# Flags times edge weights, moved from VectorE to ScalarE column by column, in the sort that runs beside the gathers

## The chip, the cores and the metric

The kernel runs on one core of a Trainium2 chip. The metric is the device time of one execution in microseconds (us). Before the change the median of three runs is 1511.99 us (1509.66 to 1513.52). Engines are named as the profile names them: PE (TensorE), PEld (its weight loads), DVE (VectorE), ACT (ScalarE), POOL (GpSimd), SP (SyncE).

## The reference

A graph layer over 6250 nodes of 256 features and 106,250 weighted edges is followed by an attention block. The part that matters here is the edge sum:

```
support = layernorm(x) @ W;  r_D = sigmoid(support @ a2);  gated = r_D * support
msg = gated[dst] * edge_weight[:, None]
out = segment_sum(msg, src, N);  sumnorm = segment_sum(edge_weight * r_D[dst], src, N)
out = out / sumnorm[:, None]     # then leaky/elu, residual, layernorm, sliced attention
```

## The kernel before

**Whole.** The 6250 rows of `gated` are written to DRAM (`gated_rows_dram`) in 49 blocks of 128. The edges are sorted on the chip into 49 buckets by their target block. Then, tile by tile (128 edges), POOL issues an indirect DMA that gathers 128 rows of 257 numbers, and PE multiplies them with a selection matrix S that holds the edge weights. Every bucket has at first six "head" tiles (294 in all), and later its remaining ones.

**The sort.** The 832 edge columns (128 edges each) are worked in 26 groups `g` of 32 columns, each in two halves `h` of 16. For a group:

- DVE `flag(g)`: an 0/1 matrix `flags4[g%2]` in bf16 that says for each edge and each of 49 buckets whether it belongs there. It lies bucket by bucket, with 34 elements (68 bytes) from one bucket to the next for a fixed edge column.
- PE `above(g)`: counts over the partitions; ACT `front(g)` (L1360) copies them back into the flags; DVE `ranks`, `counts`; PE `quads`, `total`; DVE `quad`.
- DVE `values(g, h)` (L845): for each of 16 columns `hot_v[h][:, j, 0, :]` = flags times the packed index (source and row), and `hot_v[h][:, j, 1, :]` = flags times the edge weight. These are two instructions of 16x49 = 784 elements a half, four a group.
- DVE `hot(g, h)` (L885): the one-hot rank matrix `hot_s[h]`.
- PE `put(g, h)`: 16 products `hot_v` x `hot_s` into a bank (32 matmul records of 128x80 in the profile).
- ACT `runs_out(g)` (L1367) copies the bank out, and POOL `send(g, 0)` and `send(g, 1)` (L664) write it to the sorted list in DRAM.

**The stretch "beside the gathers".** From group G1 + 1 = 7 on, the first 280 head tiles are gathered and summed while the sort goes on, 14 or 15 per group. Nothing is scheduled at run time: each engine has a written order, and the semaphores tie them.

- POOL in group g: 9 gathers (L676), `send(g-1, 0)`, 4 gathers, `send(g-1, 1)`, the rest of the gathers.
- PE in group g (below T0 to T3 are four shares of 3 or 4 gathered tiles): T0, `quads(g)`, `total(g)`, `above(g+1)`, T1, `put(g, 0)`, T2, `put(g, 1)`, T3.
- DVE in group g: `ranks(g)`, `counts(g)`, `flag(g+1)`, `place(g-1)` (L893, waits until `send(g-2, 0)` has landed), S matrices, a copy of indices and weights to PSUM (L1029), `values(g, 0)`, S, `values(g, 1)`, `quad`, `hot(g, 0)`, S, `hot(g, 1)`, S.
- ACT in group g: `runs_out(g-1)`, then for each share T0 to T3 `evac`: when the third tile of a bucket is summed, a copy of the bank (L1411), and behind it ACT itself issues the DMA that stores the sum (L1413). From tile 147 on, that is from group 17 on, it also issues the load of an older sum (L1417), and PE adds that sum back with two more matmul records. After T0, ACT does `front(g+1)`.

PE may start a new sum only when the bank two sums back has been copied out (`s_evac`). A gather into one of 18 row slots waits for the sum of the tile that used it (`s_seg`).

After `send(25, 1)` SP loads the sorted lists, and POOL gathers all the other tiles (L757) to the end of the graph layer.

Of the kernel before, what the change touches and what calls it, by code (L numbers as in the profile page):

```python
# [28 lines left out]
ACT = mybir.ActivationFunctionType  # L29
# [24 lines left out]
GC = 32  # L54
HC = GC // 2
# [4 lines left out]
G1 = 6  # L60
# [41 lines left out]
def build(nc, x, src, dst, ew, W, a1, a2, W_fx, b_fx, W_x, b_x, W_slice, b_slice, W_q, W_k, W_v,  # L102
          W_out, b_out, temp, out, gtab, srt, ovs):
    with ExitStack() as ctx:
# [3 lines left out]
        def sem(name):  # L108
            return ctx.enter_context(nc.semaphore(name))
# [32 lines left out]
        packew = carve(2 * EC)  # L142
        packf, ewf = packew[:, 0:EC], packew[:, EC:2 * EC]
# [39 lines left out]
        hot_v = [carve(HC * VB).rearrange("p (j v b) -> p j v b", v=2, b=NB) for k in range(2)]  # L183
# [4 lines left out]
        flags4 = [halved(t) for t in flags]  # L188
# [5 lines left out]
        vals2 = bank[4][:, 0:2 * GC].rearrange("p (v j) -> p v j", j=GC)  # L194
# [51 lines left out]
        zcol = sb("zcol", [P, 1])  # L246
# [83 lines left out]
        s_flag = sem("s_flag")  # L330
# [8 lines left out]
        s_quad = sem("s_quad")  # L339
        s_hs = sem("s_hs")  # L340
        s_hv = sem("s_hv")
        s_put = sem("s_put")
        s_out = sem("s_out")
        s_run = sem("s_run")
# [174 lines left out]
        def share(g, late):  # L519
            lo, hi = (max(0, n - late) for n in early[g])  # L520
            cuts = [lo + (hi - lo) * i // 4 for i in range(5)]
            return [range(cuts[i], cuts[i + 1]) for i in range(4)]
# [260 lines left out]
        def _(dve):  # L783
            step = Chain(dve, s_dve)
            v = nc.vector
# [42 lines left out]
            def flag(g):  # L828
                k = g % 2
                if g >= 2:  # L830
                    dve.wait_ge(s_base, g - 1)
                step(v.tensor_tensor(flags4[k][:, :, :, 1:HS],
                                     hib[:, g * GC:(g + 1) * GC].rearrange("p (h j) -> p h j", h=2).unsqueeze(1)
                                     .broadcast_to([P, NB, 2, HC]),
                                     buckets, ALU.is_equal))
                v.tensor_tensor(folded[k], flags4[k][:, :, :, 1:HC // 2 + 1], flags4[k][:, :, :, HC // 2 + 1:HS],
                                ALU.add).then_inc(s_flag, 1)

            def values(g, h):
                k = g % 2  # L840
                if g:
                    dve.wait_ge(s_put, g * 2 + h - 1)
                for i, t in enumerate((packf, ewf)):
                    w = vals2[:, i, h * HC:(h + 1) * HC] if g > G1 + 1 else t[:, g * GC + h * HC:g * GC + (h + 1) * HC]
                    m = v.tensor_tensor(hot_v[h][:, :, i, :],  # L845
                                        flags4[k][:, :, h, 1:HS].rearrange("p b j -> p j b"),
                                        w.unsqueeze(2).broadcast_to([P, HC, NB]), ALU.mult)
                m.then_inc(s_hv, 1)
# [164 lines left out]
            for g in range(2, NG):  # L1013
                tiles = share(g, SLAG) if g >= G1 else [()] * 4
                if g == G1 + 1:
                    for k in range(4):
                        dve.wait_ge(s_gd[k], 16 * len(range(k, NB, 4)))
                    decode1(0, CH * KA, 0)
                    step(v.tensor_copy(reset2, reset[:, 0:25 * HS]))
                ranks(g)  # L1020
                pair(g, 0)
                counts(g)
                if g + 1 < NG:
                    flag(g + 1)
                place(g - 1)
                pair(g, 1)
                select1(tiles[0])
                if g > G1 + 1:
                    step(v.tensor_copy(vals2, packew.rearrange("p (v n) -> p v n", v=2)[:, :, g * GC:(g + 1) * GC]))  # L1029
                values(g, 0)  # L1030
                pair(g, 2)
                select1(tiles[1])
                values(g, 1)
                pair(g, 3)
                quad(g)
                hot(g, 0)
                select1(tiles[2])
                pair(g, 4)
                hot(g, 1)
                pair(g, 5)  # L1040
                if g == 4:
                    bias()
                if g == G1 + 1:
                    decode1(CH * KA, NB * KA, 1)
                if g == G1 + 8:
                    decode1(NB * KA, NT1, 2)
                select1(tiles[3])
# [17 lines left out]
            for i in range(2):  # L1065
# [4 lines left out]
                m = v.tensor_scalar(neededi[:, 2 * i + 1, :], sumf, 16.0, None, ALU.mult)  # L1070
# [210 lines left out]
            for c in range(2):  # L1281
                m = v.tensor_scalar(Mn[:, c, :], bank[2 + c // 2][:, (c % 2) * F:(c % 2 + 1) * F], nrm[:, 1, c:c + 1], None,
                                    ALU.mult)
# [32 lines left out]
            for lo in (0, G):  # L1316
                m = v.tensor_tensor(ad[lo:lo + G, :, lo:lo + G], al[lo:lo + G, :, :],
                                    nrm[lo:lo + G, 2, :].unsqueeze(2).broadcast_to([G, NP2, G]), ALU.mult)
# [25 lines left out]
        def _(act):  # L1344
            a = nc.scalar
            a.preload_act_table_set("natural_log_exp_and_others")
            step = Chain(act, s_act)
# [7 lines left out]
            def front(g):  # L1355
# [3 lines left out]
                    act.wait_ge(s_cp, g - 1)  # L1359
                a.copy(flags4[k][:, :, :, 0], bank[0][:, 0:2 * NB].rearrange("p (b h) -> p b h", h=2)).then_inc(s_bs, 1)  # L1360

            def runs_out(g):
                k = g % 2
                act.wait_ge(s_put, g * 2 + 2)
                if g >= 2:
                    act.wait_ge(s_run, g * 32 - 32)
                a.copy(runs[k], run_bank(g)[0:VB, 0:2 * RUN]).then_inc(s_out, 1)  # L1367
# [35 lines left out]
            def evac(ns):  # L1403
                for n in ns:
                    if n % KA == KA - 1:
                        i = n // KA
                        k = i % 2
                        act.wait_ge(s_seg, n + 1)
                        if i >= 2:
                            act.wait_ge(s_pd[k], 16 * (i // 2))  # L1410
                        a.copy(ovr[:, k, :], bank[6 + k][:, 0:GW]).then_inc(s_evac, 1)  # L1411
                        act.wait_ge(s_evac, i + 1)
                        act.dma_start(ovs[:, i % NB, :], ovr[:, k, :]).then_inc(s_pd[k], 16)  # L1413
                        b = i - (NB - 3)
                        if 0 <= b < NB:
                            act.wait_ge(s_pd[b % 2], 16 * (b // 2 + 1))
                            act.dma_start(back[b % 3], ovs[:, b, :]).then_inc(s_back[b % 3], 16)  # L1417
# [10 lines left out]
            for i in range(3):  # L1428
                m = a.copy(bxc3[:, :, i], bxc[:, :])
# [14 lines left out]
            for g in range(G1 + 1, NG):  # L1444
                runs_out(g - 1)
                for i, ns in enumerate(share(g, LAG)):
                    evac(ns)
                    if i == 0 and g + 1 < NG:
                        front(g + 1)
# [66 lines left out]
            for c in range(2, NP2):  # L1516
                m = a.activation(Mn[:, c, :], bank[3][:, (c % 2) * F:(c % 2 + 1) * F], ACT.Identity, bias=zcol[:, 0:1],
                                 scale=nrm[:, 1, c:c + 1])
# [29 lines left out]
        def _(pe):  # L1548
# [24 lines left out]
            def put(g, h, lo=0, hi=HC):  # L1573
                if lo == 0:
                    pe.wait_ge(s_hv, g * 2 + h + 1)
                    pe.wait_ge(s_hs, g * 2 + h + 1)
                for j in range(lo, hi):
                    m = mm(run_bank(g)[0:VB, h * RUN:(h + 1) * RUN], hot_v[h][:, j, :, :].rearrange("p v b -> p (v b)"),
                           hot_s[h][:, j, :], j == 0, j == HC - 1)
                if hi == HC:  # L1580
                    m.then_inc(s_put, 1)
# [65 lines left out]
            for k in range(2):  # L1647
                for c in range(NP2):
                    t = nc.tensor.transpose(bank[6 + k][:, c * P:(c + 1) * P], Wxr[:, k, c // 2, (c % 2) * P:(c % 2 + 1) * P], ident[:, :])
                t.then_inc(s_wxt, 1)  # L1650
            pe.wait_ge(s_wxc, 3)
            for c in range(NP2):
                for k in range(2):
                    mm(bank[4 + k][:, c * P:(c + 1) * P], WxT[:, c, k * P:(k + 1) * P], Ws2[:, :])
                m = mm(bank[3][0:3, c * P:(c + 1) * P], bxc3[:, c, :], Ws2[:, :])
# [46 lines left out]
            with pe.If_ne(slow, 0):  # L1702
# [9 lines left out]
                for c in range(2):  # L1712
                    w = OV // 2
                    m = mm(bank[1 + c][0:1, 0:w], ones[0:NB, 0:1], ge[0:NB, c * w:(c + 1) * w])
# [118 lines left out]
            for c in range(NP2):  # L1833
                for f in range(2):
                    nc.tensor.transpose(bank[4 + f][:, c * P:(c + 1) * P], Mn[:, c, f * P:(f + 1) * P], ident[:, :])
                t = nc.tensor.transpose(bank[6][0:1, c * P:(c + 1) * P], nrm[:, 2, c:c + 1], ident[:, :])
# [3 lines left out]
            for c in range(NP2):  # L1840
# [4 lines left out]
                m = mm(o, bfx[:, cs], nbT[:, cs], False, True)  # L1845
# [3 lines left out]
            for c in range(NP2):  # L1849
                mm(bank[4][:, c * P:(c + 1) * P], W3[:, 0, :], tokd[:, c, :])  # L1850
                mm(bank[5][:, c * G:(c + 1) * G], W3[:, 1, :], tokc[:, c, :])
                m = mm(bank[6][:, c * P:(c + 1) * P], tokd[:, c, :], W3[:, 2, :])
# [3 lines left out]
            for c in range(NP2):  # L1856
                m = mm(bank[7][:, c * G:(c + 1) * G], qd[:, c, :], kc[:, c, :])
# [3 lines left out]
            for c in range(NP2):  # L1861
                t = nc.tensor.transpose(bank[4][:, c * P:(c + 1) * P], ad[:, c, :], ident[:, :])
# [3 lines left out]
            for c in range(NP2):  # L1866
                m = mm(bank[5][:, c * P:(c + 1) * P], vd[:, c, :], aT[:, c, :])
# [3 lines left out]
            for c in range(NP2):  # L1871
                m = mm(bank[6 + c // 2][:, (c % 2) * F:(c % 2 + 1) * F], oT[:, c, :], Wo[:, c, :])
# [46 lines left out]
```

## Time and profile before

| | us |
|---|---|
| median of 3 runs | 1511.99 |
| profiled execution | 1510.68 |
| its span | 1508.9 |
| PE busy in the span | 1215.9 |
| DVE busy | 1084.6 |
| ACT busy | 387.3 |
| POOL busy | 907.6 |

The profile cuts the span in 40 slices of 37.7 us. The sort beside the gathers fills slices 6 to 17 (about 195 to 640 us). "Busy" of POOL is the time of its DMA instructions, with 0.3 us between two of them that is booked as "issue". PE works at one of two clocks, 1.2 and 2.4 GHz; the profile shows the granted clock as a fraction of the higher one (0.50 or 1.00, or a mean of both over a stretch).

### The profile page before, as it was taken

To read this page: it belongs to the slowest core of one execution; us is meant where nothing else is said; L and a number is where in the kernel's file an instruction comes from. 1 tells how busy PE (TensorE), PEld (TensorE's weight loads), DVE (VectorE), ACT (ScalarE), POOL (GpSimd) and SP (SyncE) were. 2 spreads that over 40 slices of the span, in tenths; PEclk is the share of its full clock that TensorE was granted. 3 is DMA by queue.
4 is the path that set the end of the run, shared out by engine and by line. 5 is a ranking of instruction groups with operands and counts; after the bars stand their busy time and mean duration, and the time that the engine had idled before them with its cause. 6 is when DMAs were issued, how large, how long until landed. Compare 5 with 4: busy or idle time off the path is not lost.

```text
span 1508.9 us, 21356 instructions
## 1 busy us (share of the span) xinstructions
PE 1215.9 (81%) x6049; PEld 894.5 (59%) x6049; DVE 1084.6 (72%) x2779; ACT 387.3 (26%) x1221; POOL 907.6 (60%) x920
## 2 busy tenths in 40 slices
PE   4198867778788888768888888888888888888998
PEld 3187666567677777534555455545545555456787
DVE  8976799999989998435776766767676677665322
ACT  1066500111111111001332332333233333323232
POOL 0110167777777777767777777777777777770000
PEclk9599878898898989878999998999999999999999
DMA  8011144446455555556444445444444444441022
GB/s 260 2 51 61 59 66 122 120 123 126 122 148 144 153 148 162 150 117 121 111 116 115 113 116 114 117 113 114 114 111 116 113 116 116 111 112 50 23 75 72
DMA packets 158676, 166.45 MB, mean 110 GB/s; under 512 B 84287, under 2 KB 129235, under 8 KB 158572
## 3 DMA queue, kind: packets, MB, share of 16 engines
q0 software_dynamic: 42848, 114.59, 28.8%
q1 hardware_dynamic: 94556, 31.24, 9.0%
q10 hardware_dynamic: 21168, 19.35, 4.2%
q8 instruction: 50, 0.82, 0.2%
q14 instruction: 54, 0.44, 0.1%
HBM read 136.73 MB, written 28.38 MB: 109 GB/s over the span
## 4 chain that ended last, share of the span: by engine, by line
PE 30%; POOL 22%; DMA 16%; issue 14%; DVE 13%; POOLq 2%; SPq 1%; ACT 1%; DVEq 0%; ACTq 0%
PE bank L1550 29%; POOL rows L757 16%; DMA rows<-gated_rows_dram,ring_i 10%; POOL rows L676 6%; DVE big L845 5%; DMA sorted_edges_dram<-big,idx 4%; DVE big L885 2%; DMA res<-in_x_dram 2%; POOLq L749 2%; DVE S L1010 1%; DVE big L854 1%; SPq L545 1%; DVE big L858 0%; DVE big L959 0%; DVE big L872 0%
## 5 line engine op out<-in xcount | busy, mean ns | idle before, releaser
L1550 PE MATMUL bank<-rows,S 128*128 128x257 f32 (+1 forms) x2254 | 643.1, 408 | 133.7 <-DMA rows<-gated_rows_dram,ring_i 107.8
L757 POOL DMA_INDIRECT rows<-gated_rows_dram,ring_i x564 | 541.4, 960 | 178.0 <-issue 154.5
L1550 PEld LDWEIGHTS bank<-rows,S 128*128 128x128 f32 x2254 | 408.0, 197 | 327.1 <-DMA rows<-gated_rows_dram,ring_i 205.4
L676 POOL DMA_INDIRECT rows<-gated_rows_dram,lg x294 | 297.6, 1012 | 97.3 <-issue 75.9
L1550 PE MATMUL bank<-big 128*98 128x80 f32 (+2 forms) x1741 | 200.9, 283 | 96.8 <-DVE big L885 90.6
L1550 PEld LDWEIGHTS bank<-big 128*98 128x98 f32 (+1 forms) x1741 | 196.2, 201 | 110.3 <-issue 108.1
L1178 DVE TENSOR_SCALAR S<-iota,lof,srec 128x128 f32<-128x128 f32 x637 | 177.9, 351 | 1.5 <-PE bank L1550 1.3
L664 POOL DMA_INDIRECT sorted_edges_dram<-big,idx x52 | 67.7, 1302 | 178.7 <-ACT big L1367 94.8
L1189 DVE TENSOR_TENSOR ag<-bank,ovr 128x257 f32<-128x257 f32 x49 | 20.9, 428 | 196.0 <-PE bank L1550 196.0
L1411 ACT COPY ovr<-bank 128x257 f32<-128x257 f32 x98 | 36.7, 374 | 326.7 <-PE bank L1550 323.1
L1550 PE MATMUL bank<-Wxs,xT 128*128 128x512 f32 x196 | 111.5, 697 | 0.1
L845 DVE TENSOR_TENSOR big<-big,bank 128x784 f32<-128x784 bf16 x72 | 107.3, 1531 | 0.6
L1550 PE MATMUL bank<-xn,lg 128*128 128x256 f32 x392 | 101.5, 383 | 0.0
L1550 PE MATMUL bank<-big,lg 128*128 128x128 bf16 (+4 forms) x492 | 63.7, 282 | 46.6 <-issue 25.7
L1456 ACT ACTIVATE bc<-bc 128x1 f32<-128x1 f32 x49 | 9.9, 203 | 309.1 <-DVE bc L1218 309.1
L1010 DVE TENSOR_SCALAR S<-iota,lg,srec 128x128 f32<-128x128 f32 x294 | 83.3, 356 | 0.8 <-issue 0.8
L1550 PEld LDWEIGHTS bank<-xn,lg 128*128 128x128 f32 x392 | 75.8, 194 | 10.8
L1550 PEld LDWEIGHTS bank<-big,lg 128*128 128x128 bf16 x492 | 40.9, 106 | 62.8 <-issue 26.6
L1496 ACT ACTIVATE big<-bank,zcol 128x128 f32<-128x128 f32 (+1 forms) x196 | 68.2, 357 | 1.4 <-PE bank L1550 1.4
L858 DVE TENSOR_TENSOR_SCAN big<-bank,big 128x425 bf16<-128x425 f32 x72 | 67.7, 1002 | 0.0
L1334 DVE TENSOR_TENSOR S<-bank,res 128x256 f32<-128x256 f32 x49 | 20.8, 424 | 64.6 <-PE bank L1550 64.6
L1550 PEld LDWEIGHTS bank<-Wxs,xT 128*128 128x128 f32 x196 | 37.2, 210 | 40.7 <-issue 40.3
(236 smaller groups left out, 1369.8 us busy)
## 6 DMA issues: line engine op xcount, KB each, us to landing
overflow_sums_dram<-ovr ACTq DMA_DIRECT2D x98, 128.5 KB
rows<-gated_rows_dram,ring_i POOLq DMA_INDIRECT x564, 2.8
gated_rows_dram<-rows SPq DMA_DIRECT2D x49, 128.5 KB, 2.6
ovr<-overflow_sums_dram SPq DMA_DIRECT2D x49, 128.5 KB
res<-in_x_dram SPq DMA_DIRECT2D x1, 6144.0 KB
out_dram<-S SPq DMA_DIRECT2D x48, 128.0 KB, 1.7
rows<-gated_rows_dram,lg POOLq DMA_INDIRECT x294, 3.0
xn<-overflow_sums_dram ACTq DMA_DIRECT2D x33, 128.5 KB, 3.0
```

The source lines that it names most:

```text
L664: pool.indirect_dma_start(srt[:, :], bass.IndirectOffsetOnAxis(ap=idx[:, k, h:h + 1], axis=0), runs[k][:, h * RUN:(h + 1) * RUN], None).th ...
L676: pool.indirect_dma_start(rows[:, turn(n), :], None, gtab[:, :], bass.IndirectOffsetOnAxis(ap=ring1[:, n:n + 1], axis=0)).then_inc(s_row[t ...
L749: return pool.to_reg(pool.value_load(neededi[0:1, i, b:b + 1], min_val=0, max_val=1))
L757: pool.indirect_dma_start(rows[:, slot(b, u), :], None, gtab[:, :], bass.IndirectOffsetOnAxis(ap=ring_i[:, b // CH % 2, n:n + 1], axis=0)) ...
L845: m = v.tensor_tensor(hot_v[h][:, :, i, :], flags4[k][:, :, h, 1:HS].rearrange("p b j -> p j b"), w.unsqueeze(2).broadcast_to([P, HC, NB]) ...
L858: m = v.tensor_tensor_scan(run[:, lo * HS:lo * HS + n], reset2[:, 0:n], flags[k][:, lo * HS:lo * HS + n], 0.0, ALU.mult, ALU.add)
L885: v.tensor_tensor(hot_s[h], r.unsqueeze(2).broadcast_to([P, HC, RUN]), iota1[:, 0:RUN].unsqueeze(1).broadcast_to([P, HC, RUN]), ALU.is_equ ...
L1010: v.tensor_scalar(S[:, turn(n), :], iota[:, :], lof1[:, n:n + 1], srec[:, 1, n:n + 1], ALU.is_equal, ALU.mult).then_inc(s_S, 1)
L1178: v.tensor_scalar(S[:, S_slot(b, u), :], iota[:, :], lof[:, b // CH % 2, n:n + 1], srec[:, 1, NT1 + b * TQ + u:NT1 + b * TQ + u + 1], ALU. ...
L1411: a.copy(ovr[:, k, :], bank[6 + k][:, 0:GW]).then_inc(s_evac, 1)
L1496: m = a.activation(swt[:, c, b * P:b * P + n], bank[7][:, c * P:c * P + n], ACT.Identity, bias=zcol[:, 0:1], accum_out=nacc[:, c, b:b + 1])
L1550: return nc.tensor.matmul(o, l, r, start=start, stop=stop, skip_group_check=True)
```

## The change

From group 7 on, `values` makes only the product with the packed index on DVE. The product with the edge weight is made by ACT in `weighted(g, lo, hi)`, 8 columns ahead of each `evac`, so 32 instructions of 128x49 a group. Each reads one column of flags (49 elements, 68 bytes apart) and writes 49 contiguous f32, with two per-partition operands: the weight as scale and a zero column as bias. A new semaphore `s_he` counts finished halves; PE's `put(g, h)` waits for it, and DVE's `flag(g)` waits for it before it writes over the flags. The copy to PSUM takes the indices alone.

```diff
             def flag(g):
                 if g >= 2:
                     dve.wait_ge(s_base, g - 1)
+                if g - 2 > G1:
+                    dve.wait_ge(s_he, (g - 2 - G1) * 2)
...
             def values(g, h):
-                for i, t in enumerate((packf, ewf)):
+                for i, t in enumerate((packf, ewf)[0:1 if g > G1 else 2]):
...
-                    step(v.tensor_copy(vals2, packew.rearrange("p (v n) -> p v n", v=2)[:, :, g * GC:(g + 1) * GC]))
+                    step(v.tensor_copy(vals2[:, 0, :], packf[:, g * GC:(g + 1) * GC]))
...
+            def weighted(g, lo, hi):
+                k = g % 2
+                for n in range(lo, hi):
+                    h, j = divmod(n, HC)
+                    if n == lo:
+                        act.wait_ge(s_flag, g + 1)
+                    if j == 0 or n == lo:
+                        act.wait_ge(s_put, g * 2 + h - 1)
+                    m = a.activation(hot_v[h][:, j, 1, :], flags4[k][:, :, h, 1 + j], ACT.Identity, bias=zcol[:, 0:1],
+                                     scale=ewf[:, g * GC + n:g * GC + n + 1])
+                    if j == HC - 1:
+                        m.then_inc(s_he, 1)
...
             for g in range(G1 + 1, NG):
                 runs_out(g - 1)
                 for i, ns in enumerate(share(g, LAG)):
+                    weighted(g, i * 8, i * 8 + 8)
                     evac(ns)
...
             def put(g, h, lo=0, hi=HC):
                     pe.wait_ge(s_hv, g * 2 + h + 1)
                     pe.wait_ge(s_hs, g * 2 + h + 1)
+                    if g > G1:
+                        pe.wait_ge(s_he, (g - G1 - 1) * 2 + h + 1)
```

ACT's order in a group of the first half, before; L1367 is `runs_out`, L1360 `front`, and L1411 with L1413 one copied and stored sum:

```order
L1367 COPY big<-bank1 98x160 [waits s_run,s_put]
L1411 COPY ovr<-bank6 128x257 [waits s_pd0,s_seg]
L1413 DMA overflow_sums_dram<-ovr 128x257 [waits s_evac]
L1360 CAST big<-bank0 128x98 [waits s_cp,s_base]
L1411 COPY ovr<-bank7 128x257 [waits s_pd1,s_seg]
L1413 DMA overflow_sums_dram<-ovr 128x257 [waits s_evac]
L1411 COPY ovr<-bank6 128x257 [waits s_pd0,s_seg]
L1413 DMA overflow_sums_dram<-ovr 128x257 [waits s_evac]
L1411 COPY ovr<-bank7 128x257 [waits s_pd1,s_seg]
L1413 DMA overflow_sums_dram<-ovr 128x257 [waits s_evac]
```

The same group after the change, where the lines are 3 and 16 higher (L1383 `runs_out`, L1363 `front`, L1427 and L1429 the sum) and L1373 is `weighted`:

```order
L1383 COPY big<-bank1 98x160 [waits s_run,s_put]
L1373 ACTIVATE big<-big,zcol 128x49 [waits s_put,s_flag]
L1373 ACTIVATE big<-big,zcol 128x49 x7
L1427 COPY ovr<-bank6 128x257 [waits s_pd0,s_seg]
L1429 DMA overflow_sums_dram<-ovr 128x257 [waits s_evac]
L1363 CAST big<-bank0 128x98 [waits s_cp,s_base]
L1373 ACTIVATE big<-big,zcol 128x49 [waits s_put,s_flag]
L1373 ACTIVATE big<-big,zcol 128x49 x7
L1427 COPY ovr<-bank7 128x257 [waits s_pd1,s_seg]
L1429 DMA overflow_sums_dram<-ovr 128x257 [waits s_evac]
L1373 ACTIVATE big<-big,zcol 128x49 [waits s_put,s_flag]
L1373 ACTIVATE big<-big,zcol 128x49 x7
```

Eight columns now stand ahead of the first, second and third copy, and (past the end of the piece) eight more ahead of the last.

PE's order around the two `put` of a group, after the change (before, the two rows with `s_he` wait for `s_hs,s_hv` alone):

```order
L1567 MATMUL bank<-big 98x80 [waits s_he,s_hs,s_hv]
L1567 MATMUL bank<-big 98x80 x15
L1567 MATMUL bank<-rows,S 128x257 [waits s_S,s_row12,s_evac]
L1567 MATMUL bank<-rows,S 128x257 [waits s_S,s_row13]
L1567 MATMUL bank<-rows,S 128x257 [waits s_S,s_row14]
L1567 MATMUL bank<-rows,S 128x257 [waits s_S,s_row15,s_evac]
L1567 MATMUL bank<-big 98x80 [waits s_he,s_hs,s_hv]
L1567 MATMUL bank<-big 98x80 x15
```

Nothing moves on PE: T2 stands between `put(g, 0)` and `put(g, 1)` as before, and each `put` has one more semaphore to wait for.

## Rows read from the trace of the kernel before

**Rows 1.** The page, part 2: POOL busy in tenths, 40 slices.
```profile
POOL 0110167777777777767777777777777777770000
```
**Rows 2.** Waits of POOL, 240 to 660 us: us in total, times, longest.
```profile
POOL rows L676 <- issue: 70.1, 230, 0.3
```
**Rows 3.** Waits of DVE and of PE, 240 to 660 us.
```profile
DVE idx L893 <- DMA sorted_edges_dram<-big,idx: 34.2, 15, 7.0
...
PE bank L1550 <- DVE big L885: 60.0, 17, 5.6
```
**Rows 4.** Timeline: start us, us, engine, line; first and last `runs_out`, last `send` pair.
```profile
221.47 0.29 ACT L1367 COPY big<-bank 98x160 f32<-98x160 f32 x1 [2.38 <-PE bank L1550]
...
618.98 0.29 ACT L1367 COPY big<-bank 98x160 f32<-98x160 f32 x1 [1.17 <-issue]
...
628.03 0.99 POOL L664 DMA_INDIRECT sorted_edges_dram<-big,idx  x1 [0.30 <-issue]
```
**Rows 5.** Groups by line and shape, DVE and PE, 250 to 850 us.
```profile
L1550 PE MATMUL bank<-big 128*98 128x80 f32 x1088 | 131.9, 295 | 60.0 <-DVE big L885 60.0
...
L845 DVE TENSOR_TENSOR big<-big,bank 128x784 f32<-128x784 bf16 x66 | 98.3, 1531 | 0.5
...
L885 DVE TENSOR_TENSOR big<-bank,lg 128x1280 f32<-128x1280 f32 x34 | 50.4, 1481 | 0.0
```
**Rows 6.** ACT by line and shape; the first by its own line, min/median/max ns; a timeline pair.
```profile
L1373 ACT ACTIVATE rows<-res,big x49: 583/590/652, 58.2 to 176.7; 128x256 f32<-128x256 f32 x49
...
151.14 1.08 ACT L1373 ACTIVATE rows<-res,big 128x256 f32<-128x256 f32 x2
...
L1411 ACT COPY ovr<-bank 128x257 f32<-128x257 f32 x94 | 35.2, 374 | 314.5 <-PE bank L1550 310.9 <-DMA overflow_sums_dram<-ovr 2.6
...
L1360 ACT CAST big<-bank 128x98 bf16<-128x98 f32 x16 | 9.4, 588 | 42.5 <-PE bank L1550 42.5
...
L1493 ACT COPY big<-bank 128x88 f32<-128x88 f32 x1 | 0.2, 232 | 2.5 <-PE bank L1550 2.5
```
**Rows 7.** PE's timeline, one late group, from behind one `put(g-1, 1)`.
```profile
485.39 1.07 PE L1550 MATMUL bank<-rows,S 128*128 128x257 f32 x4
...
494.64 2.97 PE L1550 MATMUL bank<-big 128*98 128x80 f32 x32 [0.73 <-DVE big L885]
497.45 0.64 PE L1550 MATMUL bank<-ag,ident 128*128 128x257 f32 x2
...
500.10 2.92 PE L1550 MATMUL bank<-big 128*98 128x80 f32 x32
```
**Rows 8.** ACT's timeline in the same group.
```profile
487.81 0.29 ACT L1367 COPY big<-bank 98x160 f32<-98x160 f32 x1 [0.94 <-ACT ovr L1411]
...
500.20 0.45 ACTq L1417 DMA_DIRECT2D ag<-overflow_sums_dram  x1
```
**Rows 9.** PE's and ACT's timeline, one early group.
```profile
243.13 3.25 PE L1550 MATMUL bank<-rows,S 128*128 128x257 f32 x14
...
245.06 0.29 ACT L1367 COPY big<-bank 98x160 f32<-98x160 f32 x1 [0.45 <-ACT ovr L1411]
...
245.95 0.33 ACTq L1413 DMA_DIRECT2D overflow_sums_dram<-ovr  x1
```
**Rows 10.** A slower `put` behind a wait, and the clock granted in it and in a later one.
```profile
474.39 5.59 PE L1550 MATMUL bank<-big 128*98 128x80 f32 x32 [4.12 <-DVE big L885]
...
474.50:480.00 5.50, 5.50 (x33) 5.50 (x34) 5.50 (x11) 0.00 (x0) 4.14 (x5) 0.50 0.38 102
500.20:502.80 2.60, 2.60 (x33) 2.60 (x32) 2.57 (x5) 0.00 (x0) 1.99 (x3) 1.00 0.69 196
```
**Rows 11.** Timeline of group 7, and POOL's gathers by shape, 250 to 850 us.
```profile
205.33 3.43 POOL L676 DMA_INDIRECT rows<-gated_rows_dram,lg  x1 [0.30 <-issue]
...
205.00 2.98 DVE L845 TENSOR_TENSOR big<-big 128x784 f32<-128x784 bf16 x2
...
L676 POOL DMA_INDIRECT rows<-gated_rows_dram,lg x266 | 259.4, 975 | 81.0 <-issue 69.1 <-PE bank L1550 6.1 <-DMA sorted_edges_dram<-big,idx 4.3
```

More of the change, by code:

```diff
@@ L341, in build @@
         s_hv = sem("s_hv")
+        s_he = sem("s_he")
         s_put = sem("s_put")
```

## The prediction

> **What bounds the kernel now.** I read the page first, then the waits of the stretch in which the sort runs beside the gathers, then one group of it in the order of time.
>
> POOL is busy seven tenths in nearly every slice from the start of the gathers to the end of the graph layer [rows 1]. The rest is not waiting: in 240 to 660 us the idle time ahead of its gathers is 0.3 us between any two, 230 times, put down to "issue" [rows 2]. So POOL issues without a pause, and what another engine does more quickly changes nothing unless POOL was waiting for it. DVE itself is held by POOL: 34.2 us it waits for a `send` to land [rows 3]. PE waits 60.0 us, 17 times, for `hot` [rows 3], about 3.5 us a group. It runs ahead of POOL, though: `runs_out(25)` stands at 618.98, and POOL comes to `send(25, 0)` only at 628.03 [rows 4]. So PE and ACT can fall back by 9.0 us before POOL waits for them at the end of the sort. From 221.47, `runs_out(7)`, to 618.98 are 18 groups, 22.08 us each [rows 4]. Break-even is therefore a ring of PE and ACT of 22.08 + 9.0/18 = **22.6 us a group**. Everything behind the sort waits for the last `send` and shifts with it.
>
> **What the change takes away.** Two of four `values` instructions a group, 1531 ns each [rows 5]: 3.1 us of DVE in 19 groups, 58 us in all, and a shorter copy. For the time this is worth nothing in groups 8 to 25, since DVE already waits for POOL; it waits longer in `place`, and `hot` is ready 3 us earlier. In group 7 alone both operands of `values` lie in SBUF, and one gather issued beside it took 3.43 us where the mean is 0.975 [rows 11]. Two instructions less there give POOL back about 2 x 1.5 = 3 us. They might also give nothing (other work fills the gap).
>
> The skill's page on SBUF (Trainium skill, "SBUF — State Buffer", section "SBUF: two separate sides") says that DVE with two SBUF inputs and GpSimd share a port pair that one holds for its whole instruction. The slow gather beside `values` agrees; by that rule, too, groups 8 and later give nothing, because one operand is in PSUM there.
>
> **What it adds on ACT.** 32 instructions a group. The trace has no such one, so I bound it. A pair of L1373 (256 elements, SBUF to SBUF, scale and bias per partition) takes 1.08 us, one 0.59, so 0.49 from start to start [rows 6]. An element costs (374 - 232)/(257 - 88) = 0.84 ns [rows 6]. With 49 elements instead of 256: 0.49 - 207 x 0.84 ns = **0.32 us**, the lower end, if the 68-byte steps cost nothing. For the steps there are two rows. DVE reads the same flags in L845 at 1531/784 = 1.95 ns an element, against 1481/1280 = 1.16 in L885 [rows 5]: 0.8 ns more, over 49 elements 0.04 us, so 0.36 us. ACT itself writes bf16 34 bytes apart in L1360: 588 ns for 98 elements, where 232 + 10 x 0.84 = 240 would be due [rows 6]. That is 3.55 ns an element, over 49 elements 0.17 us, so **0.49 us**, the upper end. I take 0.36, since that row reads these very data; L1360 writes. Eight columns (call them W) then take 8 x 0.36 + 0.1 for the end = 3.0 us; at the ends 2.65 and 4.05.
>
> The same page of the Trainium skill, in its box on cachelines, says that SBUF has 16-byte lines and that each access in a new line pays a penalty, which here is every element. It gives no price; the two rows agree that there is one. Without it the sum would go by 0.32, with it by more.
>
> In work alone ACT has room: 32 x 0.36 = 11.5 us and some 7 of its own in 22 (five copies with their issues at 1.25, `front` 0.6, `runs_out` 0.3). What counts is the order: ACT makes the last eight columns only after it has copied a sum out of T2, which PE has only after `put(g, 0)`, and PE cannot begin `put(g, 1)` before.
>
> **The ring, late groups (17 to 25)** [rows 7, 8], counted from 485.39, when `put(g-1, 1)` is done:
> - `runs_out` ends at 488.10: +2.7. First W: 5.7.
> - Copy and two DMA issues: 0.37 + 0.33 + 0.45 and 0.1 of gaps = 1.25 [rows 6, 8, 9]: 7.0. `front` 0.59, 0.1 of it overlapped [rows 6]: 7.5. Second W: 10.5. PE had T1 behind it at 494.64 - 0.73 = 493.91, +8.5, so it now waits 2.0.
> - `put(g, 0)` 497.45 - 494.64 = 2.8: 13.3. T2 500.10 - 497.45 = 2.65: 15.95.
> - The copy of T2 and its issues end at 500.65, 0.55 behind T2: 16.5. Last W and a semaphore: 19.6. PE waits 3.65.
> - `put(g, 1)` 2.8: **22.4 us**.
>
> That is with PE at full clock. The `put` behind a wait of 4.12 us took 5.59 us at a granted clock of 0.50 (1.2 GHz); one without a wait took 2.92, in a stretch at 1.00 [rows 10]. Over the 34 `put` of rows 5, two a group cost 131.9/17 = 7.76 us, so the one behind the wait 4.84, 1.9 more than the other. The wait for `hot` goes; a wait of 3.65 us before the other `put` takes its place, and 2.0 before the first. I add 1.9 once: **24.3 us**.
>
> **Early groups (8 to 16)** [rows 9], from 243.13: `runs_out` ends at +2.2, W 5.2, copy with one issue 0.8: 6.0, `front` 6.5, W 9.5, `put` 12.3, T2 four tiles at 3.25/7 = 0.46, 14.1, tail at most 0.55, W and semaphore 17.7, `put` 20.5, with the slower clock **22.4 us**.
>
> **Sum.** Lag behind the old pace of 22.1: 9 x 0.3 + 9 x 2.2 = 22.5 us, less the 9.0 of lead: 13.5 us. The 3 us of group 7 don't come off, because PE and ACT then set the end of the sort, not POOL. 1510.68 + 13.5 = 1524.2; the median of the runs lies 1.3 above the profiled execution: **1525 us**. DVE's new wait in `flag(g+2)` for the last eight columns of g holds its `place`, S matrices and `values(g+1)` up to near the end of `put(g, 1)`. Of these the two `values` are 3.1 us [rows 5], and I estimate the rest at as much again; PE wants `hot(g+1, 0)` only 10 us after that `put`, so I count it as nothing; were that cover gone, it would add up to 1 us a group.
>
> **Rivals.**
> - **POOL stays the bound** (other side: no change). If eight columns take 2.65, the ring is 1.05 less: 21.4 and 23.3, a lag of 9 x 1.2 = 11 against 9.0; if the waits don't lower the clock, late groups take 22.4 and lag 3. The sort then ends at POOL's pace, less 3 us from group 7 at best: 1509 to 1514. It decides at 22.6 us a group. For it: waits of PE are only moved, and the lead in the middle of the sort is larger than at its end. Against it: two waits a group where there was one.
> - **Strided reads cost ACT what its strided writes cost.** W is 4.05, three of them are in the ring: +3.15. Early 25.6, late 27.5, lag 9 x 3.5 + 9 x 5.4 = 80, less 9.0: 1510.68 + 71 + 1.3 = 1583. For it: the only strided row of ACT. Against: that is a 2-byte write, and DVE's read pays far less.
> - **DVE's relief reaches POOL everywhere.** If each of the 266 gathers of rows 11 became 3% shorter and the ring stayed under 22.6, that is 8 us: 1504. For it: POOL is the bound and group 7 shows that DVE can slow it. Against: the removed instructions read one operand from PSUM from group 8 on.
>
> **How the numbers follow.** Forecast 42% (own range 1515 to 1545, about half a microsecond a group either way), POOL stays the bound 26%, dear strided reads 25%, relief of POOL 7%. A difference under 0.3% (4.5 us) can't be told from no change. Faster is the last case: 0.07. No change is most of the first rival: 0.24. Slower is the rest: 0.69. The range is 1507 to 1585: it leaves out the relief and the upper half of the dear reads beyond 1583, under 2 in 10.
>
> **What would show it.** Right: 608 new ACT instructions of 0.45 to 0.5 us in the profile, 0.36 from start to start; PE waits for ACT instead of `hot`, twice a group and longer before `put(g, 1)`; `runs_out` 23 to 24 us apart in late groups; POOL waits for ACT or PE ahead of the last `send`, which comes some 13 us later; the stretch behind it unchanged in length. Wrong: POOL still with nothing but "issue" ahead of it, or columns at 0.5 us from start to start, or DVE as the one that PE waits for.

## The result, and the profile after

The changed kernel takes 1561.97 us (median of 4 runs, 1560.64 to 1564.36), the kernel before 1511.45 beside it: ratio 1.0324, 95% interval [1.031, 1.0337]. It is 50.5 us slower where the forecast was 13.5. In the profile of the changed kernel the lines of `values`, `hot` and `put` are L848, L888 and L1567, `runs_out` is L1383, a copied sum L1427, its DMA issues L1429 and L1433, `send` L665, and `weighted` L1373.

The waits in 200 to 720 us of the kernel after (engine and line, what it waited for, us in total, times, longest); they answer to [rows 2, 3], which cover 240 to 660 us of the kernel before:

```profile
POOL rows L677 <- issue: 68.6, 225, 0.3
POOL rows L677 <- PE bank L1567: 62.6, 55, 5.5
POOL sorted_edges_dram L665 <- ACT big L1383: 9.7, 1, 9.7
...
PE bank L1567 <- ACT big L1373: 118.5, 38, 5.1
...
DVE big L835 <- ACT big L1373: 83.5, 17, 7.1
```

POOL, which stood no longer than 0.3 us before any of these gathers [rows 2], now waits 62.6 us for PE, up to 5.5 at a time, and 9.7 for the last `runs_out`. PE waits for ACT, twice a group, instead of for `hot`. DVE, which waited 34.2 us for a `send` to land, now stands 83.5 us in `flag`, behind ACT's columns.

The new instructions, by their own line (min/median/max ns), and the first, a middle and the last `runs_out` of the stretch with the last `send(25, 0)`; they answer to [rows 4, 6]:

```profile
L1373 ACT ACTIVATE big<-big,zcol x608: 451/455/498, 201.5 to 669.4; 128x49 f32<-128x49 bf16 x152
...
225.30 0.29 ACT L1383 COPY big<-bank 98x160 f32<-98x160 f32 x1 [5.77 <-PE bank L1567]
...
440.31 0.29 ACT L1383 COPY big<-bank 98x160 f32<-98x160 f32 x1 [0.45 <-ACT ovr L1427]
...
679.10 0.29 ACT L1383 COPY big<-bank 98x160 f32<-98x160 f32 x1 [1.10 <-issue]
...
680.39 0.99 POOL L665 DMA_INDIRECT sorted_edges_dram<-big,idx  x1 [9.74 <-ACT big L1383]
```

`runs_out(25)` stands at 679.10 instead of 618.98, 60.1 us later; `send(25, 0)` at 680.39 instead of 628.03, 52.4 us later; the span is 53.7 longer. So the loss is made in the sort, and the rest of the kernel is little more than shifted. The nine early groups took (440.31 - 225.30)/9 = 23.9 us each, the nine late ones (679.10 - 440.31)/9 = 26.5.

One late group on PE and on ACT, from behind `put(g-1, 1)` at 514.36; it answers to [rows 7, 8]:

```profile
514.36 1.62 PE L1567 MATMUL bank<-rows,S 128*128 128x257 f32 x4
...
524.99 2.97 PE L1567 MATMUL bank<-big 128*98 128x80 f32 x32 [1.56 <-ACT big L1373]
...
530.57 0.60 PE L1567 MATMUL bank<-rows,S 128*128 128x257 f32 x2
536.21 5.59 PE L1567 MATMUL bank<-big 128*98 128x80 f32 x32 [5.04 <-ACT big L1373]
541.59 1.66 PE L1567 MATMUL bank<-rows,S 128*128 128x257 f32 x4
```
```profile
517.33 0.29 ACT L1383 COPY big<-bank 98x160 f32<-98x160 f32 x1 [0.94 <-ACT ovr L1427]
517.52 2.99 ACT L1373 ACTIVATE big<-big,zcol 128x49 f32<-128x49 bf16 x8
...
521.85 2.99 ACT L1373 ACTIVATE big<-big,zcol 128x49 f32<-128x49 bf16 x8
524.75 0.35 ACT L1427 COPY ovr<-bank 128x257 f32<-128x257 f32 x1
...
526.04 0.38 ACT L1427 COPY ovr<-bank 128x257 f32<-128x257 f32 x1 [0.94 <-ACT ovr L1427]
526.44 1.85 ACTq L1429 DMA_DIRECT2D overflow_sums_dram<-ovr  x1
528.33 0.45 ACTq L1433 DMA_DIRECT2D xn<-overflow_sums_dram  x1
528.88 2.99 ACT L1373 ACTIVATE big<-big,zcol 128x49 f32<-128x49 bf16 x8 [2.47 <-PE bank L1567]
531.78 0.35 ACT L1427 COPY ovr<-bank 128x257 f32<-128x257 f32 x1
...
533.08 2.99 ACT L1373 ACTIVATE big<-big,zcol 128x49 f32<-128x49 bf16 x8 [0.95 <-ACT ovr L1427]
```

Up to 525 us this is the forecast: the second eight columns end 10.5 us after `put(g-1, 1)`. Then the third eight begin only at 528.88, behind two copied sums with their four issues (one of them 1.85 us). PE has finished T2 at 531.2, but the copy out of T2 starts at 531.78, when those eight are through. The last eight end at 536.07, and `put(g, 1)` then runs at the lower clock.

This group is one of the slower ones. In three late groups of the nine the issue of one stored sum took 1.43, 1.85 and 1.88 us on ACT instead of 0.33, and there 11.0 to 11.3 us pass from the start of `put(g, 0)` to that of `put(g, 1)`. Four late groups have neither such an issue nor a slow `put(g, 0)`. In three of them ACT has three copied sums between its second and its last eight columns, and they need 9.7 us, as this one:

```profile
605.27 2.97 PE L1567 MATMUL bank<-big 128*98 128x80 f32 x32 [2.00 <-ACT big L1373]
...
614.98 5.59 PE L1567 MATMUL bank<-big 128*98 128x80 f32 x32 [4.53 <-ACT big L1373]
```

In the fourth (`put(18, 0)` at 475.08) only two copied sums lie there, and it needs 8.4 us.

The steps of the ring over all groups, as means of nine in us, read from PE's timeline of the kernel after as in the prediction (each step from start to start), with the prediction's own sums beside them:

| step | early, forecast | early, measured | late, forecast | late, measured |
|---|---|---|---|---|
| end of `put(g-1, 1)` to `put(g, 0)` | 9.5 | 9.53 | 10.5 | 10.99 |
| `put(g, 0)` | 2.8 | 4.38 | 2.8 | 3.27 |
| from there to `put(g, 1)` | 5.4 | 5.65 | 6.3 | 7.13 |
| `put(g, 1)` | 4.7 | 4.04 | 4.7 | 5.05 |
| whole ring | 22.4 | 23.60 | 24.3 | 26.43 |

Between two `runs_out` it is 23.9 and 26.5, since `runs_out` stands 0.2 us behind its `put` in group 7, 2.8 in group 16 and 3.7 in group 25.

### The profile page after: what moved, and what is told of

It is laid out like the page before. It is cut to its first block, busy times and chain, and to the rows that moved or that the text cites. A ratio compares the mean times of both kernels' runs of the same rounds, so it can differ in the third digit from the quotient of the medians.

```text
span 1562.6 us, 22019 instructions
## 1 busy us (share of the span) xinstructions
PE 1229.9 (79%) x6049; PEld 912.0 (58%) x6049; DVE 1030.9 (66%) x2741; ACT 601.9 (39%) x1829; POOL 908.0 (58%) x920
## 4 chain that ended last, share of the span: by engine, by line
PE 34%; POOL 15%; issue 14%; ACT 14%; DMA 11%; DVE 6%; ACTq 3%; POOLq 2%; SPq 1%; DVEq 0%
PE bank L1567 33%; POOL rows L758 15%; ACT big L1373 11%; DMA rows<-gated_rows_dram,ring_i 8%; ACTq L1429 2%; DMA res<-in_x_dram 2%; ACT ovr L1427 1%; POOLq L750 1%; DVE big L848 1%; ACTq L1433 1%; DVE big L857 1%; DVE big L888 1%; SPq L546 0%; DVE big L962 0%; PE bank L1627 0%
## 5 line engine op out<-in xcount | busy, mean ns | idle before, releaser
L1567 PE MATMUL bank<-rows,S 128*128 128x257 f32 (+1 forms) x2254 | 632.6, 406 | 124.0 <-DMA rows<-gated_rows_dram,ring_i 111.4
L1567 PEld LDWEIGHTS bank<-rows,S 128*128 128x128 f32 x2254 | 412.0, 198 | 306.3 <-DMA rows<-gated_rows_dram,ring_i 203.5
L1567 PE MATMUL bank<-big 128*98 128x80 f32 (+2 forms) x1741 | 220.6, 300 | 144.1 <-ACT big L1373 118.5
L1567 PEld LDWEIGHTS bank<-big 128*98 128x98 f32 (+1 forms) x1741 | 212.5, 216 | 162.3 <-issue 161.8
L1373 ACT ACTIVATE big<-big,zcol 128x49 f32<-128x49 bf16 x608 | 227.3, 458 | 31.2 <-ACT ovr L1427 23.9
L665 POOL DMA_INDIRECT sorted_edges_dram<-big,idx x52 | 68.2, 1311 | 186.4 <-ACT big L1383 84.5
L1567 PE MATMUL bank<-Wxs,xT 128*128 128x512 f32 x196 | 116.5, 725 | 0.1
L1567 PE MATMUL bank<-xn,lg 128*128 128x256 f32 x392 | 101.7, 384 | 0.0
L1427 ACT COPY ovr<-bank 128x257 f32<-128x257 f32 x98 | 35.8, 366 | 168.7 <-PE bank L1567 163.6
L1567 PE MATMUL bank<-big,lg 128*128 128x128 bf16 (+4 forms) x492 | 63.1, 281 | 46.3 <-issue 25.4
L1567 PEld LDWEIGHTS bank<-xn,lg 128*128 128x128 f32 x392 | 75.6, 194 | 10.8
L835 DVE TENSOR_TENSOR big<-big 128x1568 bf16<-128x1568 bf16 x26 | 25.4, 976 | 83.5 <-ACT big L1373 83.5
L1567 PEld LDWEIGHTS bank<-big,lg 128*128 128x128 bf16 x492 | 40.7, 105 | 62.2 <-issue 26.3
L1567 PEld LDWEIGHTS bank<-Wxs,xT 128*128 128x128 f32 x196 | 38.6, 218 | 43.1 <-issue 42.6
```

What stands on the lines that cost most here:

```text
L665: pool.indirect_dma_start(srt[:, :], bass.IndirectOffsetOnAxis(ap=idx[:, k, h:h + 1], axis=0), runs[k][:, h * RUN:(h + 1) * RUN], None).th ...
L835: step(v.tensor_tensor(flags4[k][:, :, :, 1:HS], hib[:, g * GC:(g + 1) * GC].rearrange("p (h j) -> p h j", h=2).unsqueeze(1) .broadcast_to ...
L1373: m = a.activation(hot_v[h][:, j, 1, :], flags4[k][:, :, h, 1 + j], ACT.Identity, bias=zcol[:, 0:1], scale=ewf[:, g * GC + n:g * GC + n + 1])
L1567: return nc.tensor.matmul(o, l, r, start=start, stop=stop, skip_group_check=True)
```

## The experiments

Ratios are to the kernel before in the same job, with 95% intervals. e1 to e4, and e13 to e19, had it at 1510.7 to 1513.6 us. Where nothing else is said, a diff is against the changed kernel. In the expectations "Theory A" is the account that I held, and the other letters are its rivals.

**e1: ACT's load without the waits.** The kernel before, plus:

```diff
+                    for n in range(i * 8, i * 8 + 8 if g > G1 + 1 or i < 3 else 24):
+                        a.activation(srec[:, n % 24 // 12, NT1 + n % 12 * NB:NT1 + (n % 12 + 1) * NB], buckets[:, :, n // HC, n % HC], ...)
                     evac(ns)
```


> The kernel before, with 8 columns of the same shape ahead of each share of copies on ACT (from a constant table with 64-byte steps, into unused memory; the last 8 of group 7 are left out), and nobody waits for them; DVE still makes both products. Theory A (the loss is PE's wait for s_he, ACT's occupancy alone is harmless): the sums are copied out up to 3 us later, PE's put is not held; between 1511 and 1516 us. Rival B (ACT's load itself is the cost: late copies hold PE's next sum and POOL's row slots): most of the 50 us, 1540 or more.

1514.15 us, ratio 1.0002 [0.9992, 1.0012]. ACT does 600 more instructions of 0.46 us and nothing is lost, as by theory A. The cost is not ACT's occupancy but who waits for it.

**e2: nobody makes the weights' products.** `values` makes the index product alone, and there is no `weighted`.

> The changed kernel without the products with the edge weights from group 7 on (nobody makes them, so the sums lack new weights). It shows what DVE's relief is worth by itself. Theory A (POOL is the bound, only group 7 gives something): 1508 to 1511 us. Rival C (DVE's relief reaches POOL's gathers everywhere): 1504 or less.

1510.62 us, ratio 0.9987 [0.9977, 0.9997]. Taking 58 us off DVE is worth 2 us by the ratio and 3 by the medians (1513.61 to 1510.62), as by theory A. Rival C, 1504 or less, is out.

**e3, e15: the last eight columns ahead of T2's copy.**

```diff
-                    weighted(g, i * 8, i * 8 + 8)
+                    cols = (0, 8, 16, 32, 32); weighted(g, cols[i], cols[i + 1])   # none where empty
```


> The changed kernel with the last eight columns moved ahead of T2's copy, so that ACT makes 8, 8, 16 and 0 ahead of the four shares. The same number of instructions. Theory A (ACT's order in series with T2 sets the ring): put(g,1) is held some 2 us instead of 4 to 5, ring 21 to 24 us a group, time 1512 to 1525. Rival B (load): stays at 1555 or more.

> The kernel of e3 again. Theory A: 0.9965 to 0.9985 of the kernel before, as in e3, if the kernel before is back at 1512 us; if it is again near 1714 us, 1.011 as in e11.

1509.93 us, ratio 0.9976 [0.9965, 0.9986]; run again as e15: 1507.20 us, 0.9979 [0.9968, 0.999]. The same 608 instructions in the same engine, eight of a group in another place, and the 50 us are gone. e3 even came out 2 us under the range of its expectation. PE's waits for ACT in e3:

```profile
PE bank L1569 <- ACT big L1373: 34.7, 18, 3.6
```

34.7 us are left, and POOL's only steady wait is "issue" again. That these 34.7 us cost nothing measurable is shown by e17, which takes them away.

**e4: flags read side by side.**

```diff
-  flags4[k][:, :, h, 1 + j]
+  flags[k][:, n * NB:(n + 1) * NB]
```


> The changed kernel, but each column instruction reads 49 adjacent bf16 flags instead of 49 that lie 68 bytes apart (so the weights' products are those of other flags). Theory A: start to start 0.32 us instead of 0.36, a W 2.65 instead of 2.99; 3 to 4 of them are in the ring, so 1.0 to 1.4 us a group and 18 to 25 us in all: 1537 to 1544. Rival D (the steps cost nothing, the 0.36 is the instruction's fixed time): unchanged, 1560.

1532.98 us, ratio 1.0126 [1.0109, 1.0143], 29 us faster than the changed kernel. Its instructions, by their own line:

```profile
L1373 ACT ACTIVATE big<-big,zcol x608: 410/414/492, 202.2 to 637.9; 128x49 f32<-128x49 bf16 x152
```

0.414 instead of 0.455 us: the 68-byte steps cost 0.041 us an instruction, 0.8 ns an element, as forecast from DVE's rows. Eight take 2.65 us instead of 2.99. But `runs_out(25)` comes 679.10 - 646.33 = 32.8 us earlier, 1.8 a group, more than the 1.0 to 1.4 of the expectation: with all four eights in the ring it would be 4 x 0.34 = 1.4. I put the other 0.4 down to the clock, which this run doesn't show by itself. The strided rival (0.17 us for the steps) and rival D (nothing for them) are out.

**e13: PE kept busy in its longest wait**, with the changed kernel again beside it (e14). The kernel had first been run as e5, beside a kernel before of 1714 us (end of this section).

```diff
                 segment1(tiles[2])
+                for _ in range(14):
+                    mm(bank[0][:, 384:512], ident[:, :], ident[:, :])
                 put(g, 1)
```


> The kernel of e5 with the changed kernel (e14) beside it. Theory A: 32 to 45 us faster than e14, put(g,1) about 2.9 us in late groups. Rival E (the clock behind the wait is cover, since ACT's order alone sets the ring): within 5 us of e14.

> The changed kernel once more, as the yardstick for e13: 1.03 of the kernel before.

1520.09 us, ratio 1.0061 [1.0046, 1.0077]; e14 1559.38 us, 1.0318 [1.0303, 1.0333]. So 39 of some 49 us are gone, with nothing changed in ACT's program, and rival E is out. (Of ACT's long DMA issues e14 has three, of 1.5 to 1.9 us, and e13 one, of 1.4, so a small part of the 39 may be theirs.) The changed kernel in its two halves of the stretch, then in one `put(g, 1)` (columns: stretch, length, PE, PEld, DVE, ACT, POOL busy, granted clock, DMA share, GB/s):

```profile
228.00:440.00 212.00, 159.12 (x1049) 140.97 (x1047) 155.70 (x299) 122.92 (x344) 152.14 (x152) 0.86 0.47 115
440.00:679.00 239.00, 178.66 (x1136) 156.78 (x1135) 149.91 (x293) 124.08 (x349) 152.42 (x151) 0.86 0.46 125
...
536.50:541.50 5.00, 5.00 (x32) 5.00 (x32) 4.93 (x13) 0.00 (x0) 2.46 (x2) 0.50 0.30 79
```

The same in e13, and its late `put(g, 1)` behind the filler on the timeline:

```profile
228.00:421.00 193.00, 167.34 (x1287) 151.15 (x1286) 154.78 (x299) 121.88 (x341) 147.32 (x150) 0.95 0.50 124
421.00:636.00 215.00, 185.00 (x1386) 166.19 (x1385) 149.32 (x291) 124.11 (x349) 154.91 (x155) 0.96 0.52 142
...
512.60:515.20 2.60, 2.60 (x31) 2.60 (x32) 2.56 (x8) 0.00 (x0) 1.99 (x3) 1.00 0.38 95
```
```profile
508.35 3.29 PE L1567 MATMUL bank<-ident 128*128 128x128 f32 x28
512.50 2.97 PE L1567 MATMUL bank<-big 128*98 128x80 f32 x32 [0.86 <-ACT big L1373]
```

The mean granted clock goes from 0.86 to 0.95 and 0.96, the `put` from 5.59 us at 1.2 GHz to 2.97 at 2.4. The early groups take 21.9 us instead of 23.9, the late ones 23.9 instead of 26.5 (`runs_out` at 224.01, 421.35 and 636.48). Most of that is in the two `put` themselves: together they take 6.5 and 6.4 us a group in e13, and 8.4 and 8.0 in e14.

**e16: group 7 given back.** The order of e3, with both products of group 7 on DVE and ACT starting at group 8.

> The kernel of e6 again, beside e15. Theory A (e3's gain comes from group 7): 2 to 4 us slower than e15. Rival C (relief of DVE in later groups): the same as e15.

1510.22 us, ratio 0.9996 [0.9987, 1.0005], against 1507.20 for e15 in the same job. Two gathers of POOL beside `values(7, h)`, first in e16, then in e15:

```profile
205.69 3.43 POOL L677 DMA_INDIRECT rows<-gated_rows_dram,lg  x1 [0.30 <-issue]
209.42 3.10 POOL L677 DMA_INDIRECT rows<-gated_rows_dram,lg  x1 [0.30 <-issue]
```
```profile
204.92 1.97 POOL L677 DMA_INDIRECT rows<-gated_rows_dram,lg  x1 [0.31 <-issue]
207.20 1.65 POOL L677 DMA_INDIRECT rows<-gated_rows_dram,lg  x1 [0.30 <-issue]
```

(3.43 + 3.10) - (1.97 + 1.65) = 2.9 us, and the times differ by 3.0, as by theory A. Within the noise, all that e3 gains comes from there, and rival C is out once more.

**e17: no column between T2 and `put(g, 1)`.**

```diff
+            weighted(G1 + 1, 0, HC)   # once, ahead of the loop over the groups
...
-                    weighted(g, i * 8, i * 8 + 8)
+                    if i < 2: weighted(g, HC + i * 8, HC + i * 8 + 8)
+                    elif g + 1 < NG: weighted(g + 1, (i - 2) * 8, (i - 2) * 8 + 8)
```


> The kernel of e7 again. Theory A (POOL is the bound once the ring is under 22.6): PE waits for ACT under 10 us in all, ratio to before 0.997 to 0.999, as e15. Rival F (the waiting that is left in the order 8, 8, 16, 0 still costs something): 0.995 or less.

1506.91 us, ratio 0.997 [0.9957, 0.9983]. PE's list of waits has none for ACT's columns any more (e15 still has 14.2 us). It is the fastest version here, but not told apart from e15: POOL is the bound of both, and rival F is out.

**e19: the kernel before with PE kept busy.** The same 14 matmuls ahead of `put(g, 0)`, behind a wait for `front(g+1)`, which reads the bank that they write. (e18, the same without that wait, gave no time: the filler and `front` could have used that bank at once.)

> The kernel before with 14 filler matmuls of 128x128 ahead of put(g,0) from group 7 on, where PE waits for hot. Theory A (a clock that falls costs only where the ring is the bound): put(g,0) about 2.9 us instead of 4.8, the time unchanged, ratio 0.998 to 1.002. Rival G (PE's clock is worth something wherever it waits): 0.99 or less.

1511.77 us, ratio 0.9987 [0.9978, 0.9996]. Its 36 `put` take 111.1 us from group 8 on, 3.1 each instead of 3.9 over [rows 5]:

```profile
L1550 PE MATMUL bank<-big 128*98 128x80 f32 x1152 | 111.1, 257 | 17.1 <-DVE big L885 17.1
```

The mean granted clock of 228 to 636 us rises from 0.88 to 0.95, the level that e13 reached, but that gives only 0.6 to 3.3 us (the interval), not 39. Rival G is out.

**Runs beside a slower kernel before.** In three jobs the kernel before took 1714 to 1716 us at a mean granted clock of 0.82 to 0.84, where it was 0.90 to 0.92 otherwise. The traces kept from these jobs, those of the kernels beside it, have waits that are put down to no event of this core ("remote"), 41.9 us of POOL's in e5 for one. In the first of them (e5 to e7) and the second (e8 to e11) the kernels of e13, e16, e17 and e3 were tried, in the third (e12) that of e13 alone.

> The changed kernel, with 14 matmuls of 128x128 f32 into an unused part of a bank between T2 and put(g,1), so that PE is busy while it waits for ACT (some 3 us of the 4 to 5). Theory A (part of the loss is the lower clock behind the wait: in late groups put(g,1) took 5.59 us at 0.50 instead of 2.92): put(g,1) takes about 2.9 us, runs_out 2 to 2.7 us closer, 36 to 45 us off the 50, so 1517 to 1530 us. Rival E (ACT's order alone sets the ring; PE's clock is cover): within 5 us of 1562, or later.

> The order 8, 8, 16, 0 of the third experiment, with group 7 as before (DVE makes both products there, ACT starts at group 8). Theory A (what this version gains over the kernel before, 0.24%, comes from two VectorE instructions fewer beside POOL's gathers in group 7): the gain is gone, ratio to before 0.999 to 1.001. Rival C (relief of DVE in the later groups): still 0.9976.

> The first 16 columns of group g+1 are made ahead of T2's and T3's copies of group g, the last 16 of g ahead of T0's and T1's, so no column stands between T2 and put(g,1). Theory A (POOL is the bound once the ring is under 22.6): PE waits for ACT under 10 us in all, and the time is that of the third experiment and of the one without weights, ratio 0.997 to 0.999. Rival F (PE's remaining 35 us of waiting for ACT still cost something): 0.995 or less.

> The kernel of e5 again, since the kernel before took 200 us longer than usual beside it. Theory A: put(g,1) about 2.9 us in late groups, 1517 to 1530 us. Rival E (PE's clock is cover): within 5 us of 1562, or later.

> The kernel of e6 again for the same reason. Theory A (the gain of the order 8, 8, 16, 0 comes from group 7): ratio to before 0.999 to 1.001. Rival C (relief of DVE in the later groups): 0.9976.

> The kernel of e7 again for the same reason. Theory A (POOL is the bound once the ring is under 22.6): PE waits for ACT under 10 us in all, ratio to before 0.997 to 0.999. Rival F (the waiting that is left in the order 8, 8, 16, 0 still costs something): 0.995 or less.

> The kernel of e3 again, beside e9 and e10, in five rounds. Theory A: 0.997 to 0.9985 of the kernel before, the same as e10 within the intervals and 2 to 4 us under e9.

> The kernel of e5 and e8 once more; both had the kernel before at 1714 us beside them, 200 us over its usual time. Theory A: put(g,1) about 2.9 us in late groups, 1517 to 1530 us. Rival E (PE's clock is cover, ACT's order alone sets the ring): within 5 us of 1562, or later.

The kernel of e13 had the ratios 1.0315 [1.0273, 1.0357], 1.0336 [1.0286, 1.0386] and 1.0289 [1.0244, 1.0333], that of e16 1.0102 [1.0052, 1.0151] and 1.0109 [1.0064, 1.0154], that of e3 1.011 [1.0068, 1.0151], that of e17 0.9971 [0.995, 0.9991] and 0.9982 [0.996, 1.0004]. Against the expectations these are misses, all but the ratios of e17's kernel (PE's waits for ACT, expected under 10 us, were 26.2 in e7). What disturbed those chips isn't known, and the changed kernel itself was never run there, so it is open what the filler gave on them, and nothing is concluded from these runs on the questions above. Two things can be said: a change that is level beside a kernel before of 1511 us may be 1% slower beside one of 1715 (e3, e16), and only e17's order, which leaves no column between T2 and `put(g, 1)`, kept level on both.

## Why the prediction was wrong

The forecast was slower, by 13.5 us, through a ring of PE and ACT over 22.6 us a group that eats 9.0 us of lead. The measured time, 1562, lies inside the range (1507 to 1585), but the forecast is too small by 37 us. That the range holds it is luck: its own part for this mechanism ended at 1545, and the rest up to 1585 stood there for dear strided reads, which e4 rules out. The mechanism was right, and the size of the ring was not.

- *DVE's relief is worth nothing but 3 us in group 7*: right (e2, e3 with e16). That the 3 us don't come off once the ring sets the end: it fits, since in the changed kernel those two gathers were already short (1.97 and 1.66 us), and POOL still stood 9.74 us ahead of its last `send`.
- *A column takes 0.36 us from start to start, eight take 3.0*: right, 2.99. The steps cost 0.04 us (e4). The rival of dear strided reads is out: 0.041 us, not 0.17.
- *The lead is 9.0 us, break-even 22.6*: right. 60.1 us of lag less 9.0 is 51.1; `send(25, 0)` moved by 52.4.
- *Group 7 counted as no loss*: wrong. `runs_out(7)` came 3.8 us later; ACT's columns held both its `put`, for 2.4 and 4.0 us.
- **The first step that failed is "I add 1.9 once", the term for the lower clock.** It let one `put` of a group be slow, by 1.9 us. The two `put` together were taken as 7.5 us and measured 8.4 in early and 8.3 in late groups. In early groups both often ran slowly (4.0 to 5.4 us), in late ones `put(g, 1)` mostly took 5.4 from start to start, 2.6 over the faster one. That is 0.8 to 0.9 us a group, 16 us in 18 groups. e13 shows what the clock did in all: 39 us, 2.0 to 2.6 a group. In the kernel before the same slow `put` was nearly free (e19).
- **The second is, in the late groups, "the copy of T2 and its issues end at 500.65, 0.55 behind T2".** The walk kept T2's copy where it stood in the kernel before. On ACT, three copied sums with their issues (1.3 us each) and the third W lie between the second W and the last one: 3 x 1.3 + 2.9 + 2.9 = 9.7 us, an estimate from the rows above, and 9.7 is what the undisturbed groups show from `put` to `put`, where the walk had 9.1. With two copied sums it would be 8.4, and the one such group shows 8.4. The walk had only one of these copies there and took the third W as hidden behind `put(g, 0)` and T2. Three groups add 1.3 to 1.6 us by the long issue. With them this step is 0.8 us a group over the forecast, 7 us in nine groups. e4 fits that all four W are in the ring, but doesn't decide it.
- What is left of the 37 us are 0.5 us a group ahead of `put(g, 0)` in the late groups (4 us), 0.3 between the two `put` in the early ones (2 us), 3.5 us by which `runs_out` fell behind its `put`, and the 3.8 of group 7. No run takes one of these away by itself.

The two main causes aren't separate shares: either repair alone takes back most, the order 52 us (e3), the clock 39 (e13), because each brings the ring to or near POOL's pace, and what lies below that pace gives nothing. The sum above says where the time stood in one trace, not what each repair is worth.

*DVE's new wait in `flag` counted as nothing*: it is 83.5 us of idle time, and PE's waits for DVE's S are 5.6 us. No run takes it away alone. e3 keeps the semaphore, but its wait is only 10.5 us there, and e13 keeps 73.3 us of it. Whether a part of the ring runs through it is open.

## What to carry to other kernels

Work that goes to an idle engine goes into that engine's order: ask for each piece what stands ahead of it there, what waits behind it, and walk one whole period of both engines again, moving every old event that the new work pushes. Room in busy time said nothing here: after the change ACT was busy in 58% and 52% of the two halves of the stretch (122.92 of 212 us, 124.08 of 239), and the place of eight of 32 instructions was worth 50 us. And where an engine without slack waits some microseconds each period, price the clock behind each wait: filler work in the wait may pay, but only if that engine is in the ring that sets the time.

## What the runs showed of the hardware

- ScalarE reading bf16 at 68-byte steps pays 0.8 ns an element over adjacent ones (0.455 and 0.414 us for 49 elements, e4). For its bf16 writes 34 bytes apart the prediction's estimate was 3.55 ns an element more [rows 6], and no run takes those steps away. The estimate was no guide to the price of the reads.
- 14 matmuls a group that compute nothing made the changed kernel 39 us faster: the mean granted clock of the sort rose from 0.86 to 0.95 (e13, timed against e14). In the kernel before, where POOL sets the pace, the clock rose from 0.88 to 0.95 and the gain was 0.6 to 3.3 us (e19).
- Three of the 98 stores that ACT issued in the changed kernel's sort held it for 1.43, 1.85 and 1.88 us, where most take 0.33. In those groups 11.0 to 11.3 us passed from `put` to `put` instead of 9.7, so on this path most of the delay was paid. What makes such an issue long isn't shown.
